# VectorE takes its maxima of the logits read back, and GpSimd its subtractions, one tile ahead

## The chip, the cores and the metric

The kernel runs on one core of a Trainium2 chip. The metric is the device time of one execution, in microseconds (us). Profile names: PE is TensorE's matmuls and PEld its weight loads, DVE is VectorE, ACT is ScalarE, POOL is GpSimd, SPq the queue on SyncE from which the loads and stores of this part are issued.

## The reference

A decoder block over x of 64 x 128 tokens with 128 features: self-attention, cross-attention, and a soft mixture of experts, each added to its input and layer-normalised. What matters here is the end of the third part:

```python
logits = (jnp.einsum('tzd,ed->tze', x, phi_w) + phi_b).reshape(t, z, n, p)   # n = 64 experts, p = 32 slots
D = jax.nn.softmax(logits, axis=3)
C = jax.nn.softmax(logits, axis=2)
X_tilde = jnp.einsum('tznp,tzd->npd', D, x)
...
Y_tilde = jnp.einsum('npd,ndH->npH', X_tilde, expert_w) + expert_b[:, None, :]
Y = jnp.einsum('tznp,npH->tzH', C, Y_tilde)
x = _layernorm(x + Y)
```

## The kernel before, in words

Five parts follow one another: self-attention, cross-attention, gathering (D, X_tilde), the experts (`run_experts`), and mixing (`mix_slots`: C, Y and the last layer norm). The change is in mixing and in the lines of `run_experts` that start it.

Mixing works through 64 tiles of 128 tokens. A tile has 128 x 2048 logits, handled as two units of 16 slots x 64 experts: unit 2t and unit 2t + 1. The logits of the even unit are computed again by TensorE into PSUM (`logits`, L1301). Those of the odd unit were stored to DRAM while gathering and are read back into one of three buffers `mix_read` (`load`, L1293).

For each tile t:

- `peaks` on VectorE: the maxima over the experts of the even unit (`mix_mx`, L1328), then those of the odd unit that was read back (`mix_high`, L1332), then the subtraction of the second half of `mix_mx` from PSUM (L1337). `shift` on TensorE (L1307) subtracts the first half with one matmul.
- `lower` on GpSimd (L1350): `mix_less` = `mix_read` - `mix_high`.
- `exponentials` on ScalarE: unit 2t from PSUM (L1316), unit 2t + 1 from `mix_less` (L1320), each into its buffer `mix_e`.
- `invert_sums` on VectorE for each unit: the sums over the experts (`mix_sums`, L1342) and their reciprocals (`mix_rinv`, L1345).
- `divide` on GpSimd for each unit: `mix_c` = `mix_e` times `mix_rinv` (L1357).
- TensorE transposes `mix_c` (`last_T`, L1432), ScalarE copies it (`last_cT`, L1441), TensorE multiplies it with the experts' outputs (`last_Y`, L1425).
- the layer norm: VectorE L1465, L1468, L1471 with a memset between, GpSimd L1488, L1491, L1493, ScalarE L1450.

Every engine's order is written out by hand in a loop over k; step k stands for unit k, and `tiles(k, lag)` gives tile (k - lag) / 2 where that is whole. VectorE does for even k = 2t: `invert_sums(2t - 1)`, `peaks(t)`; for the odd k = 2t + 1 behind it: the layer norm of tile t - 3, `invert_sums(2t)`. GpSimd does for k = 2t: the two divides of tile t - 1; for k = 2t + 1: `lower(t)`, the norm of tile t - 3. ScalarE does for k = 2t: the copy of unit 2t - 3, the output of tile t - 4; for k = 2t + 1: the copy of unit 2t - 2, the two exponentials of tile t. TensorE does for k = 2t: `logits(t)`, the products of unit 2t - 4, the transposes of unit 2t - 2; for k = 2t + 1: `shift(t)`, the products of unit 2t - 3, the transposes of unit 2t - 1. Semaphores give the rest of the order. `load(t)` waits until `lower(t - 3)` is done, since that frees its buffer. SyncE issues the loads in order with the stores of the output, each of which takes two tiles.

`run_experts` already does the work of tile 0 up to its divides, the maxima of tile 1, and issues the loads of tiles 0 and 1. The load of tile 2 is the first that `mix_slots` issues.

Of the kernel before, what the change touches and what calls it, by code (L numbers as in the profile page):

```python
# [18 lines left out]
ALU = mybir.AluOpType  # L19
ACT = mybir.ActivationFunctionType  # L20
X = mybir.AxisListType.X
F32 = mybir.dt.float32
# [10 lines left out]
EXPERTS, SLOTS = 64, 32  # L33
# [22 lines left out]
def reach(eng, sem, value):  # L56

    if not isinstance(value, int) or value > 0:
        eng.wait_ge(sem, value)  # L59
# [1044 lines left out]
def run_experts(nc, w, psX, mix):  # L1104
# [5 lines left out]
    with ExitStack() as ctx:  # L1110
# [6 lines left out]
        n = st.sb("n", [128, 16, 128])  # L1117
# [15 lines left out]
        @block.vector  # L1133
        def _(dve):
            for c in range(4):
                dve.tensor_scalar(xt[:, c, :], psX[:, c, :], 65000.0, -33000.0, ALU.min, ALU.max).then_inc(xt_ready, 1)
            def statistics(c):
                dve.wait_ge(t_made, c + 1)
                for k in PARTS[c]:
                    ins = dve.bn_stats(stats[:, k, :], psT[:, k, :])  # L1140
                ins.then_inc(st_done, 1)
                dve.wait_ge(st_done, c + 1)
                dve.memset(w.scratch[:], 0.0)
                for k in PARTS[c]:
                    ins = dve.bn_aggr(mv[:, k, :], stats[:, k, :])
                ins.then_inc(mv_ready, 1)

            def normalise(c):
                dve.wait_ge(rstd_ready, c + 1)
                dve.wait_ge(w2_ready, 2)  # L1150
                for k in PARTS[c]:
                    ins = dve.tensor_scalar(n[:, k, :], psT[:, k, :], mv[:, k, 0:1], rstd[:, k:k + 1],
                                            ALU.subtract, ALU.mult)
                ins.then_inc(n_ready, 1)

            for c in range(4):
                statistics(c)
                if c > 0:
                    normalise(c - 1)
            normalise(3)  # L1160
            mix.peaks(dve, 0)
            dve.wait_ge(w.be_loaded, 16)
            for c in range(4):
                if c == 2:
                    mix.invert_sums(dve, 0)
                if c == 3:
                    mix.invert_sums(dve, 1)
                dve.wait_ge(yT_made, c + 1)
                dve.tensor_tensor(yT.rearrange("h (p n) -> h p n", n=EXPERTS)[:, :, 16 * c:16 * c + 16],
                                  psT[:, 4 * c:4 * c + 4, :].rearrange("h k (g p) -> h p (k g)", p=SLOTS),  # L1170
                                  w.beT[:, 16 * c:16 * c + 16].unsqueeze(1).to_broadcast([128, SLOTS, 16]),
                                  ALU.add).then_inc(yT_ready, 1)
            mix.peaks(dve, 1)

        @block.gpsimd
        def _(pool):
# [88 lines left out]
class Mix:  # L1265


    TILES = TOKENS // 128
    UNITS = 2 * TILES
    READS = 3  # L1270
    EARLY = 2
# [51 lines left out]
    def peaks(self, dve, t):  # L1323
        mx = self.mx[t % 2]
        dve.wait_ge(self.l_made, t + 1)
        reach(dve, self.shifted, t - 1)
        reach(dve, self.lowered, t - 1)
        dve.tensor_reduce(mx[:].rearrange("t (i p) -> t i p", i=2),  # L1328
                          self.psL[t % 2].rearrange("t i (p n) -> t i p n", p=8), X, ALU.max).then_inc(self.mx_ready, 1)
        dve.wait_ge(self.loaded[t % self.READS], 16 * (t // self.READS + 1))  # L1330
        reach(dve, self.less_ready, t - 1)
        dve.tensor_reduce(self.high[t % 2][:], self.read[t % self.READS][:].rearrange("t i p n -> t p i n"),  # L1332
                          mybir.AxisListType.XY, ALU.max).then_inc(self.high_ready, 1)

        dve.wait_ge(self.mx_ready, t + 1)
        second = self.psL[t % 2][:, 1, :].rearrange("t (p n) -> t p n", p=8)
        dve.tensor_tensor(second, second, mx[:, 8:16].bitcast(F32).unsqueeze(2).to_broadcast([128, 8, EXPERTS]),  # L1337
                          ALU.subtract).then_inc(self.lowered, 1)

    def invert_sums(self, dve, u):  # L1340
        dve.wait_ge(self.e_ready, u + 1)
# [20 lines left out]
def mix_slots(nc, w, mix, out):  # L1362
# [4 lines left out]
    TILES, UNITS, READS, EARLY = mix.TILES, mix.UNITS, mix.READS, mix.EARLY  # L1367
    with ExitStack() as ctx:  # L1368
# [22 lines left out]
        def tiles(k, lag):  # L1391

            return [(k - lag) // 2] if (k - lag) % 2 == 0 and 0 <= k - lag < UNITS else []
# [3 lines left out]
        @block.sync  # L1397
        def _(sync):
            for t in range(TILES + 4):
                if t + READS - 1 < TILES:  # L1400
                    mix.load(sync, t + READS - 1)
                if t >= 4 and t % 2 == 0:
                    p = (t - 4) // 2
                    sync.wait_ge(res_ready, 2 * p + 2)
                    sync.dma_start(out[p * 256:(p + 1) * 256, :].rearrange("(b s) d -> s b d", b=2), res[p % 2][:])\
                        .then_inc(stored[p % 2], 16)
            for i in range(2):
                sync.wait_ge(stored[i], 16 * (TILES // 4))
# [44 lines left out]
        @block.vector  # L1453
        def _(dve):
            for k in ORDER:
                for t in tiles(k, 2):
                    if t >= 1:
                        mix.invert_sums(dve, 2 * t + 1)
                for t in tiles(k, 0):
                    if t >= EARLY:  # L1460
                        mix.peaks(dve, t)
                for t in tiles(k, 7):
                    dve.wait_ge(cT_read, 2 * t + 2)
                    reach(dve, res_ready, t - 1)
                    dve.tensor_tensor(y[t % 2][:], psY[t % 2][:, 0:128], w.xres[:, t * 128:(t + 1) * 128], ALU.add)\  # L1465
                        .then_inc(y_done, 1)
                    dve.wait_ge(y_done, t + 1)
                    dve.bn_stats(stats[:], y[t % 2][:]).then_inc(st_done, 1)  # L1468
                    dve.wait_ge(st_done, t + 1)
                    dve.memset(w.scratch[:], 0.0)  # L1470
                    dve.bn_aggr(mv[t % 2][:], stats[:]).then_inc(mv_ready, 1)  # L1471
                for t in tiles(k, 1):
                    if t >= 1:
                        mix.invert_sums(dve, 2 * t)

        @block.gpsimd
        def _(pool):
            for k in ORDER:
                for t in tiles(k, 2):
                    if t >= 1:  # L1480
                        mix.divide(pool, 2 * t)
                        mix.divide(pool, 2 * t + 1)
                for t in tiles(k, 1):
                    if t >= 1:
                        mix.lower(pool, t)
                for t in tiles(k, 7):
                    pool.wait_ge(mv_ready, t + 1)
                    pool.tensor_tensor(veps[:], mv[t % 2][:, 1:2], w.eps[:, 0:1], ALU.add).then_inc(ve_done, 1)  # L1488
                    pool.wait_ge(ve_done, t + 1)
                    reach(pool, res_ready, t - 1)  # L1490
                    pool.tensor_tensor(rstd[t % 2][:], veps[:], w.neg_half[:, 0:1], ALU.pow).then_inc(rstd_ready, 1)  # L1491
                    pool.wait_ge(rstd_ready, t + 1)
                    pool.tensor_scalar(shift[t % 2][:], mv[t % 2][:, 0:1], -1.0, rstd[t % 2][:], ALU.mult, ALU.mult)\  # L1493
                        .then_inc(shift_ready, 1)
# [6 lines left out]
def decoder_block(nc, io, out):  # L1501
    with ExitStack() as ctx:
# [58 lines left out]
        with ExitStack() as banks:  # L1561
            sl = Store(nc, banks, "slots")
            psX = sl.ps("X", [128, 4, 512])
            w.we = sl.sb("we", [128, EXPERTS, 128])
            w.beT = sl.sb("beT", [128, EXPERTS])
            gather_slots(nc, io, w, psX)
            w1_space.close()
            with ExitStack() as spaces:
                mix = Mix(nc, spaces, w, psX)
                run_experts(nc, w, psX, mix)  # L1570
                mix_slots(nc, w, mix, out)
# [32 lines left out]
```

## Time and profile before

| | |
|---|---|
| median of 3 runs | 1380.32 us (1377.62 to 1383.22) |
| the profiled execution | 1381.27 us, of which the span is 1379.2 us |
| mixing, from the entry of `mix_slots` to the end | from 926.98 us to the end of the span |
| TensorE, GpSimd, VectorE busy from 1000 to 1060 us | 60.00, 56.85, 54.85 us of 60 |

Times of instructions are counted from the start of the span. A row of the timeline gives the start, the duration, the engine, the line, the operation, what is written and read with its shape, the count of merged instructions, and in brackets the idle time of the engine ahead of it with what ended it. The end of a matmul is modelled, so TensorE is better read by the starts of its instructions.

### The profile page before, as it was taken

How to read it: one execution, taken by the hardware profiler on the slowest of the kernel's cores; microseconds unless marked ns; L12 is line 12 of the kernel's file. 1: busy time of each engine (PE TensorE's matmuls, PEld its weight loads, DVE VectorE, ACT ScalarE, POOL GpSimd, SP SyncE). 2: the span in 40 equal slices, each digit the busy share in tenths (PEclk: the TensorE clock that was granted, in tenths of full speed). 3: DMA queues.
4: the chain of work that ended last, by engine and by line, in shares of the span. 5: the costliest groups of instructions: out<-in, count | busy, mean ns of one | idle time of the engine just before them, and what ended most of it. 6: DMA issues, size and time to landing. Idle time of an engine off the chain costs nothing. (4 is left out here: it accounts for less than half of the span.)

```text
span 1379.2 us, 31693 instructions
## 1 busy us (share of the span) xinstructions
PE 1286.2 (93%) x11006; PEld 1050.8 (76%) x11006; DVE 1105.5 (80%) x2462; ACT 896.5 (65%) x1670; POOL 1162.0 (84%) x1044
## 2 busy tenths in 40 slices
PE   6785899999998799999999999969999999999998
PEld 5664677777776577777777777659999999999997
DVE  4997466666666788888888888878999999999996
ACT  3996566666666477767777677645666666666664
POOL 3666587888886599999999999958999999999997
PEclk9997899999999999999999999999999999999999
DMA  4222434434341122222222222212222222232321
GB/s 111 79 83 76 131 112 121 123 111 132 112 122 52 54 92 84 85 89 95 85 84 92 92 85 85 85 60 83 88 86 83 91 79 95 74 100 70 103 70 32
DMA packets 90963, 123.74 MB, mean 90 GB/s; under 512 B 8803, under 2 KB 62628, under 8 KB 90804
## 3 DMA queue, kind: packets, MB, share of 16 engines
q1 hardware_dynamic: 90294, 121.49, 27.9%
q8 instruction: 90, 1.47, 0.5%
q14 instruction: 67, 0.55, 0.1%
q10 hardware_dynamic: 512, 0.23, 0.1%
HBM read 70.41 MB, written 51.33 MB: 88 GB/s over the span
## 5 line engine op out<-in xcount | busy, mean ns | idle before, releaser
L1098 POOL TENSOR_TENSOR gather_d<-gather_e,gather_rinv 128x1024 f32<-128x1024 f32 x128 | 245.2, 1915 | 35.9 <-DVE gather_rinv L1077 35.9
L1357 POOL TENSOR_TENSOR mix_c<-mix_e,mix_rinv 128x1024 f32<-128x1024 f32 x128 | 241.1, 1904 | 17.9 <-DVE mix_rinv L1345 16.0
L1425 PEld LDWEIGHTS last_Y<-kept_phi,last_cT 128*128 128x128 f32 x2048 | 248.3, 192 | 7.2
L1425 PE MATMUL last_Y<-kept_phi,last_cT 128*128 128x128 f32 x2048 | 249.1, 275 | 0.0
L1441 ACT COPY last_cT<-last_T 128x1024 f32<-128x1024 f32 x128 | 128.5, 1004 | 132.4 <-PE last_T L1432 132.4
L920 POOL TENSOR_TENSOR cross_kd<-first_pack,kept_consts 128x624 fp32r<-128x624 f32 x128 | 155.7, 1238 | 59.7 <-DMA first_pack<-first_halves 54.3
L819 DVE TENSOR_REDUCE cross_mx<-cross_S 128x8 fp32r<-128x624 f32 x128 | 103.6, 809 | 107.9 <-PE cross_S L637 107.9
L1342 DVE TENSOR_REDUCE mix_sums<-mix_e 128x16 f32<-128x1024 f32 x128 | 155.8, 1217 | 34.4 <-ACT mix_e L1316 34.0
L1073 DVE TENSOR_REDUCE gather_rsum<-gather_e 128x32 f32<-128x1024 f32 x128 | 156.1, 1220 | 25.8 <-ACT gather_e L1046 25.8
L1092 POOL TENSOR_TENSOR gather_dl<-gather_d,gather_dh 128x512 fp32r<-128x512 f32 x128 | 166.3, 1299 | 0.0
L1035 ACT COPY gather_keep<-gather_L 128x256 f32<-128x256 f32 x256 | 94.8, 370 | 95.7 <-PE gather_L L1009 95.3
L1432 PE MATMUL last_T<-kept_consts,mix_c 128*128 128x128 f32 x1024 | 134.6, 275 | 3.2 <-POOL mix_c L1357 1.1
L1046 ACT ACTIVATE gather_e<-gather_L 128x1024 f32<-128x1024 f32 x128 | 131.1, 1025 | 7.4
L741 ACT ACTIVATE cross_pT<-cross_P 77x1024 f32<-77x1024 f32 x128 | 131.3, 1029 | 0.6 <-PE cross_P L657 0.6
L1023 PE MATMUL slots_X<-gather_d,kept_xres 128*128 128x512 f32 x256 | 130.7, 592 | 0.0
L1350 POOL TENSOR_TENSOR mix_less<-mix_read,mix_high 128x1024 f32<-128x1024 f32 x64 | 122.6, 1916 | 7.4 <-DVE mix_high L1332 4.1
L1432 PEld LDWEIGHTS last_T<-kept_consts,mix_c 128*128 128x128 f32 x1024 | 114.8, 142 | 4.5 <-issue 2.5
L1067 DVE TENSOR_REDUCE gather_mx<-gather_L 128x16 fp32r<-128x512 f32 x128 | 88.6, 692 | 29.6 <-PE gather_L L1009 20.7
L1028 PE MATMUL slots_X<-gather_dh,gather_x2h 128*128 128x512 f32 x128 | 101.0, 789 | 2.9 <-DVE gather_x2l L1083 1.5
L1058 ACT CAST gather_dh<-gather_d 128x512 fp32r<-128x512 f32 x128 | 79.5, 621 | 31.4 <-PE slots_X L1030 19.6
L1069 DVE TENSOR_REDUCE gather_mx<-gather_L 128x16 fp32r<-128x512 f32 x128 | 87.2, 681 | 0.0
L1009 PE MATMUL gather_L<-over_w1h,kept_xh 128*128 128x512 f32 x256 | 81.5, 400 | 4.3 <-ACT gather_e L1046 3.3
(205 smaller groups left out, 2979.6 us busy)
## 6 DMA issues: line engine op xcount, KB each, us to landing
kept_logits<-gather_keep SPq DMA_DIRECT2D x128, 256.0 KB, 2.0
mix_read<-kept_logits SPq DMA_DIRECT2D x64, 512.0 KB, 3.8
first_halves<-first_qk SPq DMA_DIRECT2D x32, 412.0 KB, 3.2
first_pack<-first_halves SPq DMA_DIRECT2D x64, 128.0 KB
first_pack<-first_halves SPq DMA_DIRECT2D x32, 206.0 KB
first_pack<-first_halves SPq DMA_DIRECT2D x64, 78.0 KB
first_xTg<-in_xT SPq DMA_DIRECT2D x16, 256.0 KB, 2.8
kept_xres<-in_x SPq DMA_DIRECT2D x16, 256.0 KB, 3.2
```

The source lines that it names most:

```text
L741: act.activation(pT[n % 2][0:J, hs, :, :], psP[:, hs, :, :], ACT.Exp)\
L920: pool.tensor_tensor(kd[n % 2][:, q], keys[:, q].to_broadcast([128, 2, 4, JP]), w.own.unsqueeze(1).unsqueeze(3).to_broadcast([128, 2, 4, J ...
L1023: pe.matmul(psX[:, 2 * j + 1, :], w.xres[:, rows(u)], dd[u % 4][:, 1, :], start=first, stop=last)\
L1046: act.activation(e[u % 2][:], psL[u % 2][:].rearrange("p i (n s) -> p i n s", n=16), ACT.Exp)\
L1073: dve.tensor_reduce(rsum[u % 2][:].rearrange("p (i n) -> p i n", i=2), e[u % 2][:], X, ALU.add)\
L1092: pool.tensor_tensor(dl[u % 2][:], dd[u % 4][:, 0, :], dh[u % 2][:], ALU.subtract).then_inc(dl_ready, 1)
L1098: pool.tensor_tensor(dd[u % 4][:].rearrange("p i (n s) -> p i n s", n=16), e[u % 2][:], rinv[u % 2][:].rearrange("p (i n) -> p i n", i=2). ...
L1342: dve.tensor_reduce(self.sums[u % 2][:], self.e[u % 2][:], X, ALU.add).then_inc(self.sum_done, 1)
L1357: pool.tensor_tensor(self.cc[u % 2][:], self.e[u % 2][:], self.rinv[u % 2][:].unsqueeze(2).to_broadcast([128, 16, EXPERTS]), ALU.mult)\
L1425: ins = pe.matmul(psY[t % 2][:, 0:128], cT[u % 2][:, c, :], w.yk[:, 8 * (u % 2) + c, :], start=(u % 2 == 0 and c == 0), stop=(u % 2 == 1 a ...
L1432: ins = pe.transpose(psT[:, c, :], mix.cc[u % 2][:, 2 * c:2 * c + 2, :], w.ident)
L1441: act.copy(cT[u % 2][:], psT[:]).then_inc(cT_ready, 1)
```

## The change

`peaks(t)` keeps the maxima in PSUM and puts their subtraction straight behind them. The maxima of the logits read back become a function of their own, `highest`, and VectorE does `highest(t + 1)` behind `peaks(t)`. GpSimd does `lower(t + 1)` where it did `lower(t)`. In `run_experts` `highest` follows `peaks` for tiles 0 and 1, and the call for tile 2 comes at k = 2, ahead of `invert_sums(2)` at k = 3.

```diff
@@ run_experts, VectorE @@
             mix.peaks(dve, 0)
+            mix.highest(dve, 0)
...
             mix.peaks(dve, 1)
+            mix.highest(dve, 1)
@@ Mix.peaks @@
                           self.psL[t % 2].rearrange("t i (p n) -> t i p n", p=8), X, ALU.max).then_inc(self.mx_ready, 1)
+        dve.wait_ge(self.mx_ready, t + 1)
+        second = self.psL[t % 2][:, 1, :].rearrange("t (p n) -> t p n", p=8)
+        dve.tensor_tensor(second, second, mx[:, 8:16].bitcast(F32).unsqueeze(2).to_broadcast([128, 8, EXPERTS]),
+                          ALU.subtract).then_inc(self.lowered, 1)
+
+    def highest(self, dve, t):
         dve.wait_ge(self.loaded[t % self.READS], 16 * (t // self.READS + 1))
         reach(dve, self.less_ready, t - 1)
         dve.tensor_reduce(self.high[t % 2][:], self.read[t % self.READS][:].rearrange("t i p n -> t p i n"),
                           mybir.AxisListType.XY, ALU.max).then_inc(self.high_ready, 1)
-
-        dve.wait_ge(self.mx_ready, t + 1)
-        second = self.psL[t % 2][:, 1, :].rearrange("t (p n) -> t p n", p=8)
-        dve.tensor_tensor(second, second, mx[:, 8:16].bitcast(F32).unsqueeze(2).to_broadcast([128, 8, EXPERTS]),
-                          ALU.subtract).then_inc(self.lowered, 1)
@@ mix_slots, VectorE @@
                 for t in tiles(k, 0):
                     if t >= EARLY:
                         mix.peaks(dve, t)
+                    if EARLY <= t + 1 < TILES:
+                        mix.highest(dve, t + 1)
@@ mix_slots, GpSimd @@
-                for t in tiles(k, 1):
+                for t in tiles(k, -1):
                     if t >= 1:
                         mix.lower(pool, t)
```

## Rows read from the trace of the kernel before

**Rows 1.** Page: busy time, share and instructions of each engine.
```profile
PE 1286.2 (93%) x11006; PEld 1050.8 (76%) x11006; DVE 1105.5 (80%) x2462; ACT 896.5 (65%) x1670; POOL 1162.0 (84%) x1044
```
**Rows 2.** The instructions that write mix_less, 943 to 1362 us: min/median/max ns, first and last start.
```profile
L1350 POOL TENSOR_TENSOR mix_less<-mix_read,mix_high x61: 1909/1916/1922, 943.3 to 1361.2; 128x1024 f32<-128x1024 f32 x61
```
**Rows 3.** Waits, 940 to 1360 us: us in total, times, longest.
```profile
DVE mix_sums L1342 <- ACT mix_e L1316: 26.5, 60, 0.7
...
POOL mix_c L1357 <- DVE mix_rinv L1345: 10.5, 46, 1.9
```
**Rows 4.** Timeline of TensorE, one tile of the steady state.
```profile
1185.01 1.08 PE L1432 MATMUL last_T<-kept_consts,mix_c 128*128 128x128 f32 x8
...
1187.93 1.04 PE L1432 MATMUL last_T<-kept_consts,mix_c 128*128 128x128 f32 x8
...
1190.21 1.95 PE L1425 MATMUL last_Y<-kept_phi,last_cT 128*128 128x128 f32 x16
1191.99 0.27 PE L1432 MATMUL last_T<-kept_consts,mix_c 128*128 128x128 f32 x1
```
**Rows 5.** Timeline of VectorE, the same tile.
```profile
1184.14 0.25 DVE L1345 RECIPROCAL mix_rinv<-mix_sums 128x16 f32<-128x16 f32 x1
1184.31 1.16 DVE L1328 TENSOR_REDUCE mix_mx<-slots_X 128x16 fp32r<-128x1024 f32 x1
1185.39 1.21 DVE L1332 TENSOR_REDUCE mix_high<-mix_read 128x16 f32<-128x1024 f32 x1
1186.52 0.69 DVE L1337 TENSOR_TENSOR slots_X<-slots_X,mix_mx 128x512 f32<-128x512 f32 x1
...
1188.38 1.22 DVE L1342 TENSOR_REDUCE mix_sums<-mix_e 128x16 f32<-128x1024 f32 x1 [0.43 <-ACT mix_e L1316]
1189.63 0.25 DVE L1345 RECIPROCAL mix_rinv<-mix_sums 128x16 f32<-128x16 f32 x1
```
**Rows 6.** Timeline of GpSimd, the same tile.
```profile
1183.04 3.77 POOL L1357 TENSOR_TENSOR mix_c<-mix_e,mix_rinv 128x1024 f32<-128x1024 f32 x2 [0.19 <-DVE mix_rinv L1345]
1186.76 1.92 POOL L1350 TENSOR_TENSOR mix_less<-mix_read,mix_high 128x1024 f32<-128x1024 f32 x1
...
1189.56 0.27 POOL L1493 TENSOR_SCALAR last_shift<-last_mv,last_rstd 128x1 f32<-128x1 f32 x1
1189.97 3.76 POOL L1357 TENSOR_TENSOR mix_c<-mix_e,mix_rinv 128x1024 f32<-128x1024 f32 x2
```
**Rows 7.** Timeline of ScalarE, the same tile.
```profile
1186.13 1.01 ACT L1441 COPY last_cT<-last_T 128x1024 f32<-128x1024 f32 x1 [1.99 <-PE last_T L1432]
1187.32 1.02 ACT L1316 ACTIVATE mix_e<-slots_X 128x1024 f32<-128x1024 f32 x1 [0.18 <-DVE slots_X L1337]
```
**Rows 8.** Timeline of the entry into mixing: SPq, VectorE, GpSimd, ScalarE.
```profile
926.98 0.32 SPq L1293 DMA_DIRECT2D mix_read<-kept_logits  x1
...
930.10 1.22 DVE L1342 TENSOR_REDUCE mix_sums<-mix_e 128x16 f32<-128x1024 f32 x1 [4.80 <-ACT mix_e L1316]
...
934.53 1.21 DVE L1332 TENSOR_REDUCE mix_high<-mix_read 128x16 f32<-128x1024 f32 x1
...
935.82 1.92 POOL L1350 TENSOR_TENSOR mix_less<-mix_read,mix_high 128x1024 f32<-128x1024 f32 x1 [0.36 <-DVE mix_high L1332]
...
936.04 1.01 ACT L1441 COPY last_cT<-last_T 128x1024 f32<-128x1024 f32 x1 [3.80 <-PE last_T L1432]
936.96 1.03 ACT L1316 ACTIVATE mix_e<-slots_X 128x1024 f32<-128x1024 f32 x1
...
946.55 3.76 POOL L1357 TENSOR_TENSOR mix_c<-mix_e,mix_rinv 128x1024 f32<-128x1024 f32 x2 [0.16 <-DVE mix_rinv L1345]
```
**Rows 9.** DMA issues, 926.9 to 927.1 us: KB each, us from issue to landing.
```profile
mix_read<-kept_logits SPq DMA_DIRECT2D x1, 512.0 KB, 4.3
```

**Rows 10.** Timeline of SPq, a load behind a store in the steady state.
```profile
1191.59 4.37 SPq L1293 DMA_DIRECT2D mix_read<-kept_logits  x2
```
**Rows 11.** The loads of mix_read, 1000 to 1300 us.
```profile
DMA to landing us min/median/max: 3.4/3.7/5.6
```

## The prediction

> **What bounds the kernel now.** I read the page first [rows 1]: TensorE is busy 93% of the span, GpSimd 84%, VectorE 80%. These are averages over five parts, so I went to the part with the change. The subtractions of tiles 3 to 63 give its beat: 61 starts from 943.33 to 1361.18 us, 60 intervals, 6.964 us a tile [rows 2]. Then the waits of that stretch [rows 3]: GpSimd waits only 10.5 us in 60 tiles for the reciprocals, VectorE 26.5 us for the exponentials. So no engine has much slack and none is named as the bound; the timelines of one tile have to say which chain closes.
>
> Three engines are near the beat. TensorE [rows 4]: transposes at 1185.01, 1187.93 and 1191.99, a tile of 6.98 us. The first transposes took 1.08 us and the second 1.04, so 0.04 of it may be a wait; what is left, 6.94 us, I read as TensorE's own work, since the products take 1.78 us from start to start however the rest shifts. GpSimd [rows 6]: divides to subtraction 3.72 us, subtraction to shift 2.80, and then the next divide at 1189.97. That one is held by VectorE: its reciprocal started at 1189.63 and took 0.25, and the divide starts 0.09 after its end. VectorE with ScalarE [rows 5, 7] is the chain that closes tightly: sums, reciprocal (1.25), sums (0.17), reciprocal (1.25), maxima in PSUM (0.17), maxima of the read logits (1.08), subtraction (1.13), the exponential 0.80 behind it (1186.52 to 1187.32), and the next sums 1.06 behind that. This makes 6.91 us. So the beat is VectorE and ScalarE at 6.91, TensorE at 6.94, GpSimd close below, with small jitter on top up to 6.964.
>
> **The change part by part.**
>
> *The subtraction in PSUM goes ahead of the maxima of the read logits.* This takes 1.13 us out of the chain above. It also puts the subtraction right behind the maxima that it waits for. In the rows an instruction that waits for nothing starts 0.08 before its predecessor's recorded end (1.16 against 1.08), one that waits for its predecessor's result 0.03 after it (1.22 against 1.25) [rows 5]. So it starts 1.19 behind the maxima, not 1.08: 0.11 us of VectorE a tile. The chain falls to 6.91 - 1.13 + 0.11 = 5.89 us. VectorE's own work grows to 6.96 - 0.43 + 0.11 = 6.64 and is no bound.
>
> Of this cost a rule speaks: the Trainium skill, "VectorE: DVE Perf Modes", section "The DRAIN you can't avoid", says that a semaphore between VectorE instructions costs nothing extra, because the pipeline is emptied anyway. By it the 0.11 would be nothing, and the new loop below would be 0.05 us a tile shorter. The two rows named differ, so I keep 0.11.
>
> *GpSimd subtracts one tile ahead.* The exponential of the odd unit no longer waits for a subtraction just made. That wait hurt little: VectorE's next sums were mostly behind the reciprocal already. What is new is what the subtraction waits for. Before, the maxima of the read logits ended at 1186.60 and GpSimd came at 1186.76 [rows 5, 6]: 0.16 us of slack. Now the subtraction of tile t + 1 stands in the same place of GpSimd's order and its maxima come later in VectorE's order, behind the subtraction in PSUM: 0.11 + 0.61 = 0.72 us later after the same reciprocal. So GpSimd waits in the middle of its tile, and behind the waiting instruction stand the norm and both divides, for which TensorE's transposes wait.
>
> The loop that this closes, start to start, goes over two tiles:
> - divide to transposes 1.97 (1183.04 to 1185.01), transposes to copy 1.12 [rows 4, 6, 7]
> - copy to exponential 0.92 (936.04 to 936.96 [rows 8]), exponential to sums 1.06 [rows 5, 7]
> - reciprocal 1.25, sums 0.17, reciprocal 1.25, maxima 0.17, subtraction 1.19 [rows 5]
> - subtraction to the maxima of the read logits 0.61 (0.69 less the 0.08)
> - these to GpSimd's subtraction 1.29, where that was waiting (934.53 to 935.82) [rows 8]
> - subtraction to the norm's shift 2.80, shift to the next divide 0.30 [rows 6]
>
> The last is the unknown: from below 0.22 (0.27 less an overlap of 0.05, as between divides and subtraction, 3.77 against 3.72), from above 0.41, where the reciprocal held it. I take 0.30, nearer to the lower, because the row at 0.41 contains that wait. The sum is 14.10 us for two tiles, 7.05 a tile (7.01 with 0.22, 7.105 with 0.41). This is above TensorE's 6.94 and 0.086 above today's beat. From the divides of tile 3 (946.55 [rows 8]) to those of tile 62 there are 59 intervals: +5.1 us.
>
> *The entry into mixing.* `highest(2)` now comes ahead of the sums of unit 2 (930.10 before [rows 8]) and waits for a load issued at 926.98 that needs 4.3 us [rows 8, 9]: it starts at about 931.35. The sums follow 1.13 later at 932.48, reciprocal 933.73. GpSimd subtracts tile 2 at 931.35 + 1.29 = 932.64 and divides 1.87 later (2.80 less the norm, which is not there yet), at 934.51. Transposes 936.48, copy 937.60, exponential 938.52 against 936.96. Sums 939.58, reciprocal 940.83, divide of tile 2 at 941.17; then sums, reciprocal, maxima, subtraction and the maxima of tile 4 at 944.22, GpSimd's subtraction 945.51, divide of tile 3 at 948.61 against 946.55: +2.1 us that nothing gives back.
>
> *The end.* The last tile has no subtraction ahead of it: the last interval is 1.97 + 1.12 + 0.92 + 1.06 + 1.25 + 0.34 = 6.66 us, below the beat. I count -0.3.
>
> *Loads.* Nothing is added. A load behind a store is issued at 1191.59 [rows 10] and was used two tiles later; now it is used one tile later, by the maxima at about 1200.3. It has 8.7 us; the longest landing is 5.6 [rows 11]. Hidden. The work for tiles 0 and 1 in `run_experts` stays beside TensorE's work there: nothing.
>
> **Sum.** 5.1 + 2.1 - 0.3 = +6.9 us. The profiled execution took 1381.27 us, so 1388.2; it lay 0.95 above the median of the runs, so 1387.2 as a median.
>
> **The rivals.**
> - *Forecast*, the new loop over GpSimd's wait: 1384.8 (7.01 a tile: 2.7 + 1.8) to 1390.4 (7.105: 8.3 + 1.8). Chance 0.58.
> - *The loop does not quite close.* Where the 0.11 is not paid and the last gap is 0.22, the loop is 6.955, and the beat is TensorE's 6.94 to 6.96. Then the steady state gains at most 1.4 us and the entry costs 1.8: 1380 to 1383. For it: every link of the loop is a single row. Against: those links held before too. Chance 0.20.
> - *Faster.* The waits for the reciprocals go and GpSimd's own work sets the beat: 3.72 + 2.80 + 0.22 = 6.74 us, a gain of 0.224 x 59 = 13.2, less 1.8: 1369. It decides if TensorE can do a tile in under 6.85 us and the maxima come before GpSimd asks. Against: rows 4 show TensorE without a gap worth more than 0.04. Chance 0.06.
> - *Slower still.* TensorE, with 0.1 us of slack a tile, has transposes queued behind products at the moment the loop needs them; each 0.1 us there costs 0.05 a tile, 3 us in all: 1390 to 1394. Chance 0.16.
>
> **How the numbers follow.** 0.5% is 6.9 us, about what the measurement can tell from no change; the forecast lies on that bound. Slower by more: 0.16 and half of 0.58, 0.45. Within: the other half and the second rival, 0.49. Faster: 0.06. The range leaves out the fast rival and half of the slow one: 1380.5 to 1391.5.
>
> **What the profile after would show.** A beat of mix_less of 7.05 us from tile 3 on; GpSimd idle some 0.5 us ahead of it in every tile, released by mix_high, and no longer idle ahead of the divides; the subtraction in PSUM 1.19 us behind mix_mx; the exponential of the even unit waiting for ScalarE's copy, not for VectorE; VectorE waiting for the load of tile 2 until 931.3 us. The prediction is wrong if mix_less does not wait for mix_high, or if TensorE's tile is seen below 6.9 us.

## The result, and the profile after

The median went from 1379.95 us to 1383.06 us (20 runs of each). The ratio of the changed kernel to the one before is 1.0025, with a 95% interval from 1.0018 to 1.0032. At 1380 us that is 3.45 us more (2.5 to 4.4). The forecast was 6.9 us more. The sign was right, the size was twice too large. In what follows the beat is the time from the work of one tile to the same work of the next, a link is the time from the start of one instruction to the start of the next one on a chain, and the entry is the stretch from GpSimd's first instruction in mixing to a named tile's divides.

The profiled execution spans 1381.7 us. First the page: busy times, and the line by which the chain that ended last runs.

```profile
PE 1289.6 (93%) x11006; PEld 1053.9 (76%) x11006; DVE 1105.3 (80%) x2462; ACT 895.9 (65%) x1670; POOL 1160.7 (84%) x1044
...
PE last_Y L1428 15%; PE last_T L1435 8%; PE slots_X L1303 6%; PE slots_X L1309 1%; POOL mix_c L1360 1%; POOL last_rstd L1496 0%; POOL mix_less L1353 0%; DVE mix_sums L1345 0%; DVE mix_high L1340 0%; DVE mix_mx L1330 0%; ACT mix_e L1318 0%; POOL last_veps L1493 0%; POOL last_shift L1498 0%; ACT last_res L1453 0%; POOLq L1371 0%
```

The page puts the end on TensorE. e6 below shows that TensorE's work does not set the beat. The waits from 940 to 1360 us (us in total, times, longest) answer to [rows 3]:

```profile
DVE mix_sums L1345 <- ACT mix_e L1318: 26.0, 60, 0.8
POOL mix_less L1353 <- DVE mix_high L1340: 13.3, 59, 1.3
POOL mix_c L1360 <- DVE mix_rinv L1348: 1.3, 1, 1.3
```

GpSimd's wait for the reciprocals is gone (10.5 us before) and a wait for `mix_high` of 13.3 us stands in its place, in 59 tiles. The forecast had both, but it gave this wait 0.5 us a tile, and 13.3 us in 59 tiles is 0.23. Its own terms said 0.23 too: 7.05 less the 3.72 + 2.80 + 0.30 of GpSimd.

Next the timeline of one loop in the steady state, from one pair of divides to the pair behind the next, and the divides of tiles 5 and 62 at its two ends.

```profile
962.60 3.77 POOL L1360 TENSOR_TENSOR mix_c<-mix_e,mix_rinv 128x1024 f32<-128x1024 f32 x2
...
1185.89 3.77 POOL L1360 TENSOR_TENSOR mix_c<-mix_e,mix_rinv 128x1024 f32<-128x1024 f32 x2
...
1187.89 1.05 PE L1435 MATMUL last_T<-kept_consts,mix_c 128*128 128x128 f32 x8
...
1188.98 1.01 ACT L1444 COPY last_cT<-last_T 128x1024 f32<-128x1024 f32 x1 [2.52 <-PE last_T L1435]
...
1189.87 1.92 POOL L1353 TENSOR_TENSOR mix_less<-mix_read,mix_high 128x1024 f32<-128x1024 f32 x1 [0.21 <-DVE mix_high L1340]
1189.89 1.03 ACT L1318 ACTIVATE mix_e<-slots_X 128x1024 f32<-128x1024 f32 x1
...
1190.95 1.22 DVE L1345 TENSOR_REDUCE mix_sums<-mix_e 128x16 f32<-128x1024 f32 x1 [0.41 <-ACT mix_e L1318]
...
1192.20 0.25 DVE L1348 RECIPROCAL mix_rinv<-mix_sums 128x16 f32<-128x16 f32 x1
1192.37 1.16 DVE L1345 TENSOR_REDUCE mix_sums<-mix_e 128x16 f32<-128x1024 f32 x1
...
1192.66 0.26 POOL L1498 TENSOR_SCALAR last_shift<-last_mv,last_rstd 128x1 f32<-128x1 f32 x1
1192.88 3.76 POOL L1360 TENSOR_TENSOR mix_c<-mix_e,mix_rinv 128x1024 f32<-128x1024 f32 x2
...
1193.57 0.25 DVE L1348 RECIPROCAL mix_rinv<-mix_sums 128x16 f32<-128x16 f32 x1
1193.74 1.16 DVE L1330 TENSOR_REDUCE mix_mx<-slots_X 128x16 fp32r<-128x1024 f32 x1
...
1194.93 0.70 DVE L1334 TENSOR_TENSOR slots_X<-slots_X,mix_mx 128x512 f32<-128x512 f32 x1
1195.54 1.21 DVE L1340 TENSOR_REDUCE mix_high<-mix_read 128x16 f32<-128x1024 f32 x1
...
1196.83 1.92 POOL L1353 TENSOR_TENSOR mix_less<-mix_read,mix_high 128x1024 f32<-128x1024 f32 x1 [0.18 <-DVE mix_high L1340]
...
1360.33 3.76 POOL L1360 TENSOR_TENSOR mix_c<-mix_e,mix_rinv 128x1024 f32<-128x1024 f32 x2
```

The beat is (1360.33 - 962.60) / 57 = 6.978 us a tile. Counted the same way, from the divides of tile 5 (960.46) to those of tile 62 (1357.46), the kernel before has 6.965. So the steady state costs 0.013 x 57 = 0.7 us, not 5. The links of the loop in these rows, start to start: 2.00, 1.09, 0.91, 1.06, 1.25, 0.17, 1.20, 0.17, 1.19, 0.61, 1.29, 2.79, 0.22 (with 1189.87 to 1192.66 for the norm). They add up to 13.95 us, 6.975 a tile.

Now the entry into mixing, which answers to [rows 8]. The load of tile 2 is issued at 926.01 (the first row merges it with a later one).

```profile
926.01 0.80 SPq L1295 DMA_DIRECT2D mix_read<-kept_logits  x2
...
926.04 1.91 POOL L1353 TENSOR_TENSOR mix_less<-mix_read,mix_high 128x1024 f32<-128x1024 f32 x1 [3.00 <-POOLq L1110]
...
929.95 1.22 DVE L1340 TENSOR_REDUCE mix_high<-mix_read 128x16 f32<-128x1024 f32 x1 [5.36 <-DMA mix_read<-kept_logits]
...
931.08 1.21 DVE L1345 TENSOR_REDUCE mix_sums<-mix_e 128x16 f32<-128x1024 f32 x1
931.25 1.91 POOL L1353 TENSOR_TENSOR mix_less<-mix_read,mix_high 128x1024 f32<-128x1024 f32 x1 [3.29 <-DVE mix_high L1340]
...
933.12 3.76 POOL L1360 TENSOR_TENSOR mix_c<-mix_e,mix_rinv 128x1024 f32<-128x1024 f32 x2
...
935.07 1.55 PE L1435 MATMUL last_T<-kept_consts,mix_c 128*128 128x128 f32 x8 [2.50 <-POOL mix_c L1360]
...
936.84 2.97 PE L1428 MATMUL last_Y<-kept_phi,last_cT 128*128 128x128 f32 x16
...
942.13 1.22 DVE L1330 TENSOR_REDUCE mix_mx<-slots_X 128x16 fp32r<-128x1024 f32 x1 [0.63 <-PE slots_X L1303]
...
948.35 3.77 POOL L1360 TENSOR_TENSOR mix_c<-mix_e,mix_rinv 128x1024 f32<-128x1024 f32 x2
```

And four stretches of it (their length, busy us of PE, PEld, DVE, ACT and POOL with counts, granted clock, DMA share, GB/s):

```profile
926.00:932.50 6.50, 5.47 (x39) 4.83 (x39) 2.52 (x4) 3.79 (x4) 3.17 (x2) 1.00 0.69 243
932.50:935.00 2.50, 0.07 (x1) 0.00 (x0) 2.46 (x4) 0.00 (x0) 2.50 (x3) 1.00 0.29 90
935.00:940.00 5.00, 4.93 (x29) 4.84 (x30) 3.18 (x5) 2.88 (x3) 3.79 (x3) 0.66 0.21 68
...
935.60:939.00 3.40, 3.40 (x18) 3.31 (x16) 1.65 (x3) 2.34 (x3) 3.19 (x2) 0.50 0.06 23
```

`mix_high` of tile 2 waits for its load, GpSimd's subtraction waits for `mix_high`, the divides stand behind it, and TensorE is idle for 2.5 us. Then the granted clock falls: it is 0.66 over 935 to 940 us and 0.50, the lower level of 1.2 GHz, from 935.6 to 939.0. The products take 2.97 us in place of 1.95. The logits of tile 3 come late, and VectorE waits 0.63 us for them, which the forecast did not have.

The kernel before has a stretch at the lower level in its entry too, earlier. Neither the rows before nor the forecast point it out. A stretch of its trace, in the same columns:

```profile
929.30:932.70 3.40, 3.40 (x12) 3.02 (x13) 2.55 (x3) 2.72 (x3) 1.01 (x1) 0.50 0.94 348
```

Its transposes there took 1.91 us; the same ones took 1.06 in the changed kernel:

```profile
929.28 1.91 PE L1432 MATMUL last_T<-kept_consts,mix_c 128*128 128x128 f32 x8 [0.98 <-ACT last_cT L1441]
```

So the entries of the two kernels differ not in whether the clock falls, but in where.

Counted from GpSimd's first instruction in mixing (927.00 before, 926.04 after), the divides come at (us, their times in the two traces in brackets):

| | before | after | more |
|---|---|---|---|
| tile 2 (939.60, 940.21) | 12.60 | 14.17 | 1.57 |
| tile 3 (946.55, 948.35) | 19.55 | 22.31 | 2.76 |
| tile 5 (960.46, 962.60) | 33.46 | 36.56 | 3.10 |
| tile 62 (1357.46, 1360.33) | 430.46 | 434.29 | 3.83 |
| tile 63 (1364.35, 1366.98) | 437.35 | 440.94 | 3.59 |

So of 3.6 us in these two traces, 3.1 arise before tile 5, 0.7 in the 57 tiles behind it, and the last interval gives 0.24 back. What lies ahead of mixing differs by 1 us between the traces, the other way, which is why the spans differ by only 2.5.

### The profile page after: what moved, and what is told of

It is laid out like the page before. It is cut to its first block and busy times, and to the rows that moved or that the text cites. A ratio compares the mean times of both kernels' runs of the same rounds, so it can differ in the third digit from the quotient of the medians.

```text
span 1381.7 us, 31693 instructions
## 1 busy us (share of the span) xinstructions
PE 1289.6 (93%) x11006; PEld 1053.9 (76%) x11006; DVE 1105.3 (80%) x2462; ACT 895.9 (65%) x1670; POOL 1160.7 (84%) x1044
## 5 line engine op out<-in xcount | busy, mean ns | idle before, releaser
L1345 DVE TENSOR_REDUCE mix_sums<-mix_e 128x16 f32<-128x1024 f32 x128 | 152.4, 1191 | 29.9 <-ACT mix_e L1318 29.9
L1046 ACT ACTIVATE gather_e<-gather_L 128x1024 f32<-128x1024 f32 x128 | 131.1, 1024 | 7.6
```

The lines of the kernel that those rows point to most:

```text
L1046: act.activation(e[u % 2][:], psL[u % 2][:].rearrange("p i (n s) -> p i n s", n=16), ACT.Exp)\
L1345: dve.tensor_reduce(self.sums[u % 2][:], self.e[u % 2][:], X, ALU.add).then_inc(self.sum_done, 1)
```

## The experiments

The theory after this reading: the forecast's loop is real but 0.07 us a tile shorter than I added it up, and the loss is mostly the late load at the entry. The rivals: the wait of GpSimd costs in every tile, or TensorE alone sets the beat and the loop is a fiction. The two theories written down ahead of e1 and e2 are these: A, TensorE sets the beat and the loss is all at the entry; B, the wait costs in every tile. e6 to e11 were one execution each (1382.76, 1375.40, 1380.88, 1383.05, 1384.29 and 1386.24 us) and are read by their traces, not by these times. The beats below are all from the divides of tile 5 to those of tile 62, the entries from GpSimd's first instruction in mixing to the divides of tile 5.

### e1: the load of tile 2 issued earlier

```diff
             mix.load(sync, 0)
             mix.load(sync, 1)
+            mix.load(sync, 2)
...
-                if t + READS - 1 < TILES:
+                if 1 <= t and t + READS - 1 < TILES:
```

> The changed kernel, with the load of tile 2 issued in run_experts instead of at the entry of mixing, so that mix_high of tile 2 waits for nothing. Theory A: the change costs nothing in the steady state, because TensorE's own work (6.96 to 6.98 us a tile) sets the beat there, and all of the 3 us arise at the entry, where mix_high of tile 2 waits for its load, the first transposes come late and every later tile inherits it. Then this run is within 0.7 us of the kernel before, and the divides of tile 3 come about 19.6 us behind the entry as before (22.3 in the changed kernel). Theory B: the new wait of GpSimd for mix_high costs about 0.05 us in each of 59 tiles, and the entry was given back. Then this run stays 2.5 to 3.5 us above the kernel before.

1381.92 us median of 11 runs, ratio 1.0012 (0.9996 to 1.0027): this interval reaches into what either theory expects. The trace tells more. GpSimd now goes straight through the subtractions of tiles 1 and 2, and the divides of tile 5 come at 961.58:

```profile
928.97 3.78 POOL L1354 TENSOR_TENSOR mix_less<-mix_read,mix_high 128x1024 f32<-128x1024 f32 x2 [2.98 <-POOLq L1110]
933.65 3.76 POOL L1361 TENSOR_TENSOR mix_c<-mix_e,mix_rinv 128x1024 f32<-128x1024 f32 x2 [0.90 <-DVE mix_rinv L1349]
...
947.61 3.76 POOL L1361 TENSOR_TENSOR mix_c<-mix_e,mix_rinv 128x1024 f32<-128x1024 f32 x2
...
961.58 3.76 POOL L1361 TENSOR_TENSOR mix_c<-mix_e,mix_rinv 128x1024 f32<-128x1024 f32 x2
```

That is an entry of 32.61 us, against 36.56 changed and 33.46 before, and tile 3 at 18.64. The beat is that of the changed kernel, 6.977. So most of the loss at the entry goes with the late load, and the beat does not depend on it. This entry is also below that of the kernel before, and that is not the load's doing: in this trace the clock was 1.00 from 929 to 961 us, while the kernel before had its stretch at 0.50. The cleaner comparison is e2 with e5 and e12, below: e5 and e12 are e2 with this edit, all three have such a stretch, and the entry is 36.13 against 33.42 and 33.41, 2.7 us.

### e2: one tile ahead, without the new order in VectorE

```diff
-    def peaks(self, dve, t):
+    def peaks(self, dve, t, ahead=None):
...
+        if ahead is not None:
+            self.highest(dve, ahead)
         dve.wait_ge(self.mx_ready, t + 1)
         second = self.psL[t % 2][:, 1, :].rearrange("t (p n) -> t p n", p=8)
...
```

(and the callers hand over the tile ahead, in place of the call of `highest` behind `peaks`.)

> One part alone: VectorE and GpSimd work one tile ahead, but the maxima of the logits read back stay between the maxima in PSUM and the subtraction in PSUM, so mix_high comes 0.7 us earlier for GpSimd than in the changed kernel. Theory A: the entry is that of the changed kernel (the load is waited for), the steady state is TensorE's: 2 to 4 us above before, with GpSimd no longer waiting for mix_high. Theory B: without the wait of GpSimd the cost goes: within 1 us of before.

1381.0 us median of 11 runs, ratio 1.0003 (0.9994 to 1.0013). Theory B's time came true (within 1 us of before), but neither theory had the reason right: the entry is as late as in the changed kernel, 36.13 us (2.67 more than before), but the beat is 6.930, below both kernels. 0.035 x 57 = 2.0 us come back. So working ahead is worth something by itself, and the new order on VectorE takes it away.

### e3: the new order in VectorE, without working ahead

```diff
-                    if EARLY <= t + 1 < TILES:
-                        mix.highest(dve, t + 1)
+                    if t >= EARLY:
+                        mix.highest(dve, t)
...
-                for t in tiles(k, -1):
+                for t in tiles(k, 1):
```

> The other part alone: the subtraction in PSUM goes ahead of the maxima of the logits read back, but both engines stay on the same tile. mix_high then comes 0.72 us later, and this loop of one tile closes: subtraction on GpSimd to exponential 2.00, to sums 1.09, reciprocal 1.20, maxima 0.17, subtraction in PSUM 1.20, mix_high 0.61, GpSimd 1.29: 7.56 us a tile. Both theories: 0.60 us in each of 61 tiles, 33 to 38 us slower than before. If it is slower by less than 10 us, sums of links read from single rows don't give a beat, and neither does the forecast's loop.

1418.41 us median of 2 runs, ratio 1.0275 (1.0256 to 1.0293), 38 us more. The beat is 7.621 us where the sum of links said 7.56. Sums of single rows do give a beat, here to 0.06 us. That is good enough for a loss of 38 us, but 0.06 x 57 is 3.4 us, as much as the whole effect of the change.

### e4: mix_high later by a known amount

```diff
                     dve.bn_aggr(mv[t % 2][:], stats[:]).then_inc(mv_ready, 1)
+                for t in tiles(k, 1):
+                    if EARLY <= t + 1 < TILES:
+                        mix.highest(dve, t + 1)
```

(taken out behind `peaks`.)

> The changed kernel with mix_high moved behind the three instructions of the layer norm on VectorE, 0.82 us later. Theory A': the loop of the forecast over two tiles exists, and with its links as the profile after shows them (last gap 0.22, second reciprocal 1.20) it is 13.95 us, 6.975 a tile, equal to TensorE's work; 0.82 us more make 7.385 a tile: 24 us slower than the changed kernel, 27 above before. Theory C: the loop has slack or isn't closed, since something else takes up the delay: less than 8 us above the changed kernel.

1407.12 us median of 2 runs, ratio 1.0193 (1.0174 to 1.0211): 27.1 us above the median before, 27 expected. From 960 to 1380 us GpSimd waits for `mix_high` 57 times, 32.0 us in all. The beat is 7.350, not the 7.385 expected, because the delay was smaller than planned:

```profile
1194.58 0.70 DVE L1334 TENSOR_TENSOR slots_X<-slots_X,mix_mx 128x512 f32<-128x512 f32 x1
...
1195.94 1.20 DVE L1340 TENSOR_REDUCE mix_high<-mix_read 128x16 f32<-128x1024 f32 x1
```

`mix_high` starts 1.35 to 1.36 us behind the subtraction, against 0.61 in the changed kernel: 0.74 later, not 0.82. Half of 0.74 is 0.37, and the beat rose by 7.350 - 6.978 = 0.372. A delay on this link goes through at half its size a tile, so the loop goes over two tiles and has no slack. The time of 27 us was met in part by luck: the beat gives 21 us over the changed kernel, and another 1.5 come from a longer entry (38.07 against 36.56).

### e6 and e7: is TensorE the bound?

Half of the products of each unit are left out, four of eight, so the output is not the reference's. e6 does this in the changed kernel, e7 in e2.

```diff
-                    for c in range(8):
+                    for c in (0, 1, 2, 7):
                         ins = pe.matmul(psY[t % 2][:, 0:128], cT[u % 2][:, c, :], w.yk[:, 8 * (u % 2) + c, :],
```

> The changed kernel with half of the products of every unit left out (4 of 8 matmul steps), which takes about 1.8 us of TensorE's work out of a tile; the output is not the reference's. Theory A (the forecast's loop over GpSimd's wait binds, 13.95 us for two tiles): the beat of mix_less stays at 6.97 to 6.98 us. Theory D (TensorE's own work binds, as the chain that ended last puts it): the beat falls below 6.9.

The beat stays: 962.66 to 1360.15 in 57 intervals, 6.974 us. TensorE now waits for the divides, and the waits from 960 to 1350 us show it, with one more thing to see:

```profile
PE last_T L1435 <- POOL mix_c L1360: 74.5, 56, 1.6
...
POOL mix_less L1353 <- DVE mix_high L1340: 11.9, 28, 0.4
```

GpSimd waits for `mix_high` in 28 of 56 tiles, every second one (0.43 us and nothing, in turn), which fits a loop over two tiles. With 1.8 us of TensorE's work gone from each tile the beat moved by 0.004. So, with e4, the loop sets it, and the page's chain through TensorE only follows one that is as long, because TensorE's work is 6.93 of the 6.978 us (the beat of e2, see e7).

> The same half of the products left out of e2. There the beat of 6.93 us should be TensorE's own work: it falls to VectorE's chain with the exponential, 1.25 + 0.17 + 1.20 + 0.17 + 1.08 + 1.13 + 0.80 + 1.06 = 6.86. If TensorE wasn't the bound: 6.93 stays.

From the divides of tile 5 to those of tile 62:

```profile
961.14 3.76 POOL L1360 TENSOR_TENSOR mix_c<-mix_e,mix_rinv 128x1024 f32<-128x1024 f32 x2
...
1352.36 3.76 POOL L1360 TENSOR_TENSOR mix_c<-mix_e,mix_rinv 128x1024 f32<-128x1024 f32 x2
```

6.864 us, 6.86 expected. In e2, then, TensorE's own 6.93 is the bound, and under it lies VectorE's chain of 6.86.

### e8: and before?

The same half of the products left out of the kernel before.

> Half of the products left out of the kernel before; the output is not the reference's. If VectorE's chain with the exponential sets its beat of 6.965 us, as its rows add up (with the waits of the second sums for the exponential of the odd unit), the beat stays within 0.02 of that. If TensorE's own 6.93 us had a part in it, it falls by 0.03 or more.

961.02 to 1357.82: 6.961 us. TensorE had 0.004 us of the beat before; VectorE's chain with ScalarE's exponentials had the rest.

### e10 and e11: does the half clock cost?

The changed kernel with 20 (e10) or 10 (e11) matmuls more, whose result nobody reads, ahead of the transposes of unit 2.

```diff
+                if k == 4:
+                    for _ in range(20):
+                        pe.matmul(psY[1][:, 0:128], w.ident, w.ident, start=True, stop=True)
                 for u in units(k, 2):
...
```

> The changed kernel with 20 matmuls more, whose result nobody reads, ahead of the transposes of unit 2, where TensorE stood idle for 2.5 us and then ran at half clock until about 939.6 us. Theory A: the late load starts the loss, and the half clock adds the rest of it: with TensorE kept busy the granted clock stays at 1.0, the transposes of unit 2 take 1.05 us and the products behind them 1.95, and the divides of tile 3 come 21.2 to 21.7 us behind the entry instead of 22.3. Theory E: the clock is not part of it: 22.3 stays.

The divides of tile 3 come at 22.78 us, so the number expected was missed: the extra matmuls took 4.5 us and held the transposes back. The clock did stay at 1.00, from 926.5 to 945 us. And from these transposes to the divides of tile 3 it is 948.98 - 937.03 = 11.95 us, against 948.35 - 935.07 = 13.28 in the changed kernel. The products between them took 1.95 us.

> As e10, with 10 matmuls in place of 20. The 20 took 4.5 us and pushed the transposes of unit 2 back by 1.7 us; 10 should take 2.2 us and fit in the idle 2.5 us. Theory A: the transposes of unit 2 start about 9.0 us behind the entry as in the changed kernel, at full clock, and the divides of tile 3 come at about 21.0 us (9.0 plus the 11.95 that e10 showed between the two), 1.3 us ahead of the changed kernel's 22.3. Theory E, the clock is no part of it: 22.3.

Missed again: 950.83 - 928.70 = 22.13. This time the lower clock came earlier, 0.50 from 931.3 to 934.7 us and so ahead of the extra matmuls, and the transposes started 10.18 us behind the entry instead of 9.0. Behind them the way is again 11.95 us (938.88 to 950.83):

```profile
930.97 1.68 PE L1438 MATMUL last_T<-kept_consts,mix_c 128*128 128x128 f32 x8 [0.97 <-ACT last_cT L1447]
...
936.65 2.40 PE L1433 MATMUL last_Y<-kept_consts 128*128 128x128 f32 x20
938.88 1.04 PE L1438 MATMUL last_T<-kept_consts,mix_c 128*128 128x128 f32 x8
```

So the same way took 13.28 us with the lower clock in it and twice 11.95 without; in e2, with the lower clock in it (0.50 from 932.6 to 936.0), it took 13.22, and in e1, without, 12.01. These are single traces, but they agree: the lower clock on this way costs 1.2 to 1.3 us. Filling the gap did not win this: in e10 the clock stayed up but the filling held the transposes back by more than it saved, in e11 the clock had fallen before. Why it falls in one trace and not in another stays open: ahead of the point where it fell in e11 the changed kernel and e10 ran the same program, and there it stayed at 1.00.

### e5, e9 and e12: the two parts that help, together

e5 and e12 are e2 with the edit of e1; e9 is the kernel before with the edit of e1.

> Both that the first two runs point to: one tile ahead with mix_high left between the maxima and the subtraction in PSUM (e2), and the load of tile 2 issued in run_experts (e1). If the entry (3.1 us by the changed kernel's trace) and the beat add up: beat 6.93 us as in e2 (0.035 below before, 2.0 us in 57 tiles), entry no longer than before: 1.5 to 3 us faster than before, ratio 0.998 to 0.999. If the beat of e2 hung on its late entry: within 1 us of before.

1378.93 us median of 11 runs, ratio 0.9987 (0.9975 to 1.0), as expected. Entry 958.40 - 924.98 = 33.42 us, with the clock at 0.50 from 927.3 to 930.7 us; beat 6.930.

> e5 a second time, on another occasion, since its interval reached to 1.0: ratio 0.998 to 0.999 against the kernel before if its trace is right (beat 6.93 against 6.965, the entry as before); 1.000 or above if the first result was chance.

The same kernel again: 1378.51 us median of 12 runs, ratio 0.9985 (0.9974 to 0.9997). Entry and end of the beat:

```profile
926.54 3.79 POOL L1354 TENSOR_TENSOR mix_less<-mix_read,mix_high 128x1024 f32<-128x1024 f32 x2 [3.06 <-POOLq L1110]
...
959.95 3.76 POOL L1361 TENSOR_TENSOR mix_c<-mix_e,mix_rinv 128x1024 f32<-128x1024 f32 x2 [0.15 <-DVE mix_rinv L1349]
...
1354.97 3.77 POOL L1361 TENSOR_TENSOR mix_c<-mix_e,mix_rinv 128x1024 f32<-128x1024 f32 x2
```

33.41 us, with the clock at 0.50 from 929.1 to 932.5 us, and 395.02 / 57 = 6.930. This version beats both kernels: by the ratios (0.9985 and 0.9987 against 1.0025), the one before by about 2 us, the changed one by about 5.

> The kernel before with the load of tile 2 issued in run_experts. There mix_high of tile 2 comes behind the sums and waits for no load: the divides of tile 5 stay at 33.4 to 33.5 us behind the entry, and the beat at 6.965. Otherwise the early load is worth something by itself, and the gain of e5 isn't that of the order.

The beat is 6.963, as expected, but the entry is 34.42 us and not 33.4 to 33.5: in this run the granted clock was 0.50 from 924.5 to 934.7 us. The trace shows no gain from the early load in the kernel before, and its beat does not move, so the gain of e5 and e12, which is in the beat, is not that of the load. The entries also differ by about 1 us where the clock differs. Where `mix_high` of tile 2 waits for its load, the entry took 36.56 (changed), 36.13 (e2) and 36.08 us (e11); where it doesn't, 33.46 (before), 32.61 (e1), 33.42 (e5), 33.41 (e12) and 34.42 (e9). With half of the products left out it is 36.02 (e6) and 34.85 (e7) against 32.49 (e8), with the extra matmuls of e10 36.73. Of the ones that don't wait, e1 and e8 are the two with no stretch at 0.50, and they are the lowest by 0.8 us and more. So the late load is worth some 2.5 to 3 us, with about 1 us of scatter by the clock.

## Why the prediction was half right

**What bounds the kernel.** Right in kind: VectorE with ScalarE bounds it before (e8), and TensorE's work of 6.93 lies close below (e2 against e7). The forecast had these two at 6.91 and 6.94 and did not say which one decides. The sum for VectorE's chain, 6.91, was 0.05 short of the beat, and I called the rest jitter. It was the wait of the second sums for the exponential of the odd unit. The row that shows it stands right behind those of [rows 5]:

```profile
1189.87 1.22 DVE L1342 TENSOR_REDUCE mix_sums<-mix_e 128x16 f32<-128x1024 f32 x1
```

It starts 0.24 behind the reciprocal at 1189.63, where the least is 0.17. Behind such a wait it is 1.25 to the reciprocal, without one 1.20, so with the wait gone the chain is 6.86 (e7). I wrote that this wait "hurt little". It was worth 0.10 us a tile (6.961 in e8 against 6.864 in e7), of which TensorE lets 0.035 through.

**The new loop.** Right in kind: it goes over GpSimd's wait for `mix_high`, over two tiles, with no slack (e4, e6). The step that failed is its size: the sum of 14.10 us for two tiles, 7.05 a tile. The rows add up to 13.95, and the beat with TensorE's products halved is 6.974 (e6). Two terms were too long. The gap from the norm's shift to the next divide is 0.22, my lower bound; I took 0.30. The second reciprocal starts 1.20 and not 1.25 behind its sums, since those now start behind VectorE's own work; the 1.25 had been read behind a wait, and only the first sums still have one. The other terms are right to 0.03. Taking 0.22 for the gap would have given 7.01, still too long: the range carried the doubt on the one term and none on the other. The beat fell from 7.05 to 6.978, and because the kernel before stands at 6.965, an error of 1% in the beat took away most of the loss: 0.7 us and not 5.1. Both signs by which the forecast called itself wrong stayed away: `mix_less` does wait for `mix_high`, and TensorE's tile is not below 6.9. They tested the kind of the loop and not its length.

**The 0.11 us between the two VectorE instructions.** Confirmed: the subtraction starts 1.19 behind the maxima. The rule of the Trainium skill weighed against it ("VectorE: DVE Perf Modes", "The DRAIN you can't avoid"), that the semaphore costs nothing extra, does not hold for these rows: an instruction behind maxima of the same size starts 1.08 behind them without the wait (1184.31 to 1185.39 in [rows 5]). Without this 0.11 the loop would be 6.92 by the sum, and TensorE's 6.93 the beat.

**The entry.** Mechanism right, size low: 3.1 us against 2.1. The wait for the load came as worked out, but `mix_high` started 3.94 us behind the issue and not 4.37. That tile 2 was 1.57 late, exactly as forecast, is luck: the transposes came 0.45 sooner than forecast, and at the lower clock the copy came 1.59 behind them and not 1.12. On the way to tile 3 VectorE waited for logits that the lower clock had made late, which cost 0.7 us that the forecast did not have (22.31 against 21.61), and another 0.3 us came between tiles 3 and 5. The way from the transposes of unit 2 to the divides of tile 3 was 1.33 us longer than in e10 and e11, where no lower clock fell on it. The forecast took a path at full clock and set it against rows of the kernel before that had a stretch at 0.50 in them; it knew of neither. The entry erred by 1 us the other way than the beat, so in the total it covered a part of the beat's error of 4.4 us.

**The end and the loads.** -0.24 against -0.3. No load was late in the steady state.

**The rivals.** The second one, that the loop does not quite close on the beat, was nearer in its steady state than the forecast (6.955 against 6.978 measured), but only a part of its reason held: the gap was 0.22, but the 0.11 was paid and the loop did close. The forecast put 6.9 us on the line between "within 0.5%" and "slower"; the result is within.

## What to carry to other kernels

Where three engines stand within a few per cent of the beat, a new loop must be summed to a few hundredths of a microsecond, and sums of single rows were off by 0.06 here (e3). Every term that is read from a row with a wait in it has to be carried as a range into the forecast, not only the one that looks doubtful. Split a change into its parts on the chip: here working ahead gains 2 us, the new order on VectorE takes it back and 0.7 more, and a call that lands ahead of its own load costs some 3 us once. When work is moved a step ahead, move the load that feeds its first use as well.

## What the runs showed of the hardware

A GpSimd instruction of 0.27 us that nothing holds is followed by the next 0.22 us after its start; one that waits for the result before it starts 0.10 after that one's end (0.55 to 0.65). The same VectorE sum over 128 x 1024 takes 1.22 us when the engine was waiting for it and 1.16 us behind other work. The granted clock was at 0.50 for a while within the first 15 us of mixing in ten of these fourteen profiles, at places that differ between them (935.6 to 939.0 us in the changed kernel, 929.3 to 932.7 in the one before, 924.5 to 934.7 in e9), and not in e1, e3, e8 and e10. In the changed kernel TensorE had stood idle for 2.5 us until 0.5 us before the fall. In the one before it had two idle gaps of 0.9 and 1.0 us shortly ahead of it; e1 has the same two gaps there and stayed at 1.00. From 945 to 1360 us it was 1.00 in the changed kernel, with TensorE busy 415 of 415 us.
